# A state-space scan whose decays move from SBUF to PSUM, in one buffer for both channel halves

## The reference, cut to what matters

```python
def step(state, xs):
    d_t, B_t, C_t, u_t = xs
    dA = jnp.exp(d_t[..., None] * A)
    state = state * dA + (d_t * u_t)[..., None] * B_t[:, None, :]
    y_t = jnp.einsum('ben,bn->be', state, C_t)
    return (state, y_t)
...
x = x + jnp.tanh(g_xattn[0]) * _L0_xattn_ref(ctx_1024, _layernorm(x, axis=-1), ...)
x = x + jnp.tanh(g_ffn[0]) * _L0_ffn_ref(_layernorm(x, axis=-1), ...)
x = x + jnp.tanh(g_xattn[1]) * _L1_xattn_ref(ctx_1024, _layernorm(x, axis=-1), ...)
```

## Time and profile before

| | us |
|---|---|
| median of three runs | 1141.84 |
| lowest, highest | 1140.94, 1142.33 |
| profiled execution, its time | 1146.28 |
| profiled execution, span | 1144.1 |
| VectorE busy | 776.8 (68%) |
| TensorE busy | 839.2 (73%) |
| GpSimd busy | 451.9 (39%) |
| ScalarE busy | 379.6 (33%) |

### The profile page before, as it was taken

One profiled execution on the slowest core, in us unless ns is written; L12 is line 12 of the kernel. 1 busy time (PEld: TensorE's weight loads), 2 busy tenths in 40 slices (PEclk: granted clock), 3 DMA queues, 4 the chain that ended last, 5 costly groups with the idle time before them and its releaser, 6 DMA issues.

```text
span 1144.1 us, 12940 instructions
## 1 busy us (share of the span) xinstructions
PE 839.2 (73%) x4202; PEld 522.8 (46%) x4202; DVE 776.8 (68%) x1130; ACT 379.6 (33%) x822; POOL 451.9 (39%) x297
## 2 busy tenths in 40 slices
PE   5797898515676768776739846689985796788993
PEld 2232333313565556554537732444442585555662
DVE  5978999798898889888965583357782835431222
ACT  1623323402333333333335510146553341202331
POOL 3015666003556555655426960033351042151332
PEclk8876888757999999899978978589998998698997
DMA  5102216440212121212010023231313401025113
GB/s 188 41 19 109 71 58 234 194 146 0 74 37 74 37 74 37 73 37 73 0 64 1 1 65 76 36 126 48 111 47 112 136 1 56 0 75 166 46 47 138
DMA packets 28674, 83.77 MB, mean 73 GB/s; under 512 B 3376, under 2 KB 17216, under 8 KB 27104
## 3 DMA queue, kind: packets, MB, share of 16 engines
q1 hardware_dynamic: 26224, 75.35, 20.4%
q0 software_dynamic: 2256, 6.18, 1.5%
q10 hardware_dynamic: 144, 1.57, 0.3%
HBM read 67.74 MB, written 19.45 MB: 76 GB/s over the span
## 4 chain that ended last, share of the span: by engine, by line
PE 42%; DVE 19%; issue 17%; POOL 11%; ACT 5%; DMA 5%; SPq 1%; DVEq 0%; POOLq 0%; ACTq 0%
PE ps L1685 6%; PE ps L511 5%; POOL M L678 5%; PE ps L1331 4%; DVE M L647 3%; PE ps L390 3%; PE ps L504 3%; PE ps L898 2%; PE ps L786 2%; DVE Z L313 2%; POOL ZT L981 2%; PE ps L1350 2%; ACT N L1756 1%; PE ps L1727 1%; DVE stats L305 1%
## 5 line engine op out<-in xcount | busy, mean ns | idle before, releaser
L786 PE MATMUL ps<-W,F 128*128 128x256 f32 x544 | 157.2, 416 | 115.7 <-DVE W L854 82.5
L786 PEld LDWEIGHTS ps<-W,F 128*128 128x128 f32 x544 | 105.8, 204 | 152.4 <-DVE W L854 104.4
L647 DVE TENSOR_TENSOR_SCAN M<-M 128x512 f32<-128x512 f32 x64 | 152.7, 2386 | 21.4 <-POOL M L678 21.4
L685 POOL TENSOR_TENSOR W<-W,M 128x1024 f32<-128x1024 f32 x32 | 75.4, 2356 | 133.6 <-DVE M L655 133.6
L589 POOL TENSOR_TENSOR M<-M 128x1024 f32<-128x1024 f32 x32 | 75.3, 2353 | 100.5 <-DVE M L465 53.6
L818 ACT ACTIVATE F<-ps 128x128 f32<-128x128 f32 x136 | 37.8, 278 | 217.9 <-PE ps L786 217.8
L1756 ACT ACTIVATE N<-ps 128x512 f32<-128x512 f32 x128 | 69.5, 594 | 106.5 <-PE ps L1689 106.5
L1685 PE MATMUL ps<-M,W 32*128 32x256 f32 x512 | 78.9, 440 | 35.3 <-DMA W<-rot_scratch 17.0
L1777 DVE TENSOR_REDUCE W<-ps 128x4 f32<-128x1024 f32 x64 | 78.1, 1221 | 23.9 <-PE ps L1685 16.5
L678 POOL TENSOR_TENSOR M<-N,M 128x1024 f32<-128x1024 f32 x32 | 89.5, 2806 | 0.0
L773 PE MATMUL ps<-W,F 128*128 128x256 f32 x272 | 84.6, 394 | 0.0
(11 more groups left out here) (272 smaller groups left out, 1768.6 us busy)
## 6 DMA issues: line engine op xcount, KB each, us to landing
M<-dbl_scratch SPq DMA_DIRECT2D x48, 512.0 KB, 3.8
W<-in_gu SPq DMA_DIRECT2D x1, 4800.0 KB, 16.3
W<-in_gu SPq DMA_DIRECT2D x1, 4352.0 KB, 14.0
att_scratch<-W SPq DMA_DIRECT2D x32, 128.0 KB
slot_scratch<-in_slots SPq DMA_DIRECT2D x1, 3999.0 KB, 19.0
M<-slot_scratch SPq DMA_DIRECT2D x3, 1032.0 KB, 9.8
W<-in_gu SPq DMA_DIRECT2D x2, 1536.0 KB, 6.9
W<-in_dn SPq DMA_DIRECT2D x1, 2176.0 KB, 18.7
```

Source lines behind the costliest of these rows:

```text
L647: nc.vector.tensor_tensor_scan(hst[:, t, at], dA[:, t, at], dBu[:, t, at], 0.0, ALU.mult, ALU.add).then_inc(S("h1_rdy"), 1)
L685: nc.gpsimd.tensor_tensor(u[1][:, t, :], u[1][:, t, :], hC[:, t, :], ALU.add).then_inc(S("y1_acc"), 1)
L786: last = nc.tensor.matmul(up, ztt[:, par, c, :], gu[:, c, s, :], start=(c == 0), stop=(c == DC - 1))
```

## The change

The second scan reads its decays from PSUM banks 0 and 1 (`dAp1`) instead of SBUF. During this stage only the router has used them before. There is one buffer for both channel halves: bank 0 holds the first half of the tokens, bank 1 the second. ScalarE therefore waits for the scan two pieces before (`g - 1` where it was `g - 3`), and at the start only the pieces of t = 0 need no wait. The zeros at the sequence starts are written to PSUM, after the router's scores have been read. The helper `decay` goes, and the first scan writes out the same operands as before.

```diff
+        dAp1 = ps[:, 0:2, :].rearrange("p a n -> p (a n)")
...
             else:
-                nc.vector.memset(dA.rearrange("p t (b l) -> p t b l", b=BATCH)[:, :, :, 0:1],
-                                 0.0).then_inc(S("delta_done"), 1)
+                dve.wait_ge(S("scores"), 1)
+                nc.vector.memset(dAp1.rearrange("p (b l) -> p b l", b=BATCH)[:, :, 0:1], 0.0).then_inc(S("delta_done"), 1)
...
-                nc.vector.tensor_tensor_scan(hst[:, t, at], dA[:, t, at], dBu[:, t, at], 0.0,
+                nc.vector.tensor_tensor_scan(hst[:, t, at], dAp1[:, at], dBu[:, t, at], 0.0,
                                              ALU.mult, ALU.add).then_inc(S("h1_rdy"), 1)
...
             g = (tile * 4 + 2 * par + t) * 2 + half
-            if not start:
-                act.wait_ge(S("h1_rdy"), g - 3)
-            v, d, _ = decay(0, t, 2 * half, 2 * half + 2)
-            scale = Acur[:, t, par:par + 1]
-            nc.scalar.activation(v, d(1), ACT.Exp, scale=scale).then_inc(S("dA1_rdy"), 1)
+            if not (start and t == 0):
+                act.wait_ge(S("h1_rdy"), g - 1)
+            b = slice(2 * half, 2 * half + 2)
+            nc.scalar.activation(batches(dAp1)[:, b, 1:], batches(delta[1][:, t, :])[:, b, 1:], ACT.Exp,
+                                 scale=Acur[:, t, par:par + 1]).then_inc(S("dA1_rdy"), 1)
```

More of the change, by code:

```diff
@@ L531, in mamba_tail_tensor @@
                 last.then_inc(S("y_tr"), 1)
[L533 to L537, removed]
+        batches = lambda v: v.rearrange("p (b l) -> p b l", b=BATCH)
         def mamba0_scalar(act):
@@ L558, in decays @@
                         act.wait_ge(S("h_rdy"), n * 2 + t)
-                    _, d, scale = decay(n, t, 0, BATCH)
-                    nc.scalar.activation(dAp.rearrange("p (b l) -> p b l", b=BATCH)[:, :, 1:], d(0), ACT.Exp,
+                    scale = Aneg[:, t, n:n + 1] if isinstance(n, int) else Aneg[:, t, bass.ds(n, 1)]
+                    nc.scalar.activation(batches(dAp)[:, :, 1:], batches(delta[0][:, t, :])[:, :, 1:], ACT.Exp,
                                          scale=scale).then_inc(S("dA_rdy"), 1)
```

## The result

The changed kernel takes 1075.64 us at the median of four runs (1071.08 to 1081.59), the kernel before 1142.09 beside it. The ratio is 0.9404, with a 95% interval of 0.9371 to 0.9437. The forecast was 1071.5 us, with a range of 1058 to 1087. The profiled execution took 1076.64 us, its span is 1074.5.

A forecast was written before the change was run, and what follows sets the result against it. VectorE bounds the stage, its second scans and GpSimd's products excluding each other when scan inputs are both in SBUF. Seven tiles at 9.05 plus tile 0's 7.00 give 70.4 us off the 1141.84 median, rounded to 1071.5; range 1058 to 1087.

The forecast's parts named there:

- The scans' held time: Second scan on VectorE: 64 scans at 1.21 us each, so 75.2 of 152.7 us held time goes.
- The tile: One of eight token tiles, 17 expert units each: 29.31 instead of 38.36 us, 9.05 less; tile 0 7.00 less.
- The start with its wait, the unit costs and the two holds: VectorE in tile 4: first scan at 5.03 us; units 1.71 with scan, 1.18 with state product; two 0.68 delays.
- The new wait: State products in units 7 and 11, two SBUF inputs, held until 0.55 us after GpSimd's drive product ends: 0.68 each.
- TensorE: Keeps up from unit 2 if its clock holds; after 2.61 us idle at tile start, the fast level was taken.
- the prediction's alternative: Slow TensorE clock: unit 5 begins at 12.05 not 10.61, unit 7's state product escapes the hold, 0.76 us a tile remains.
- ScalarE's buffer and the memset: Decay waits for the scan two pieces before, always already met; border memset waits for router scores: nothing for either.
- The sum: Whole stage: 7 x 9.05 + 7.00 = 70.4 us less; layers behind it only shift.
- No effect: Rival: scan stays held for its second input and output in SBUF, nothing moves, 1142 us; chance 0.03.
- decay in the path: Rival: single buffer puts ScalarE's decay between scans on 64 pieces, some 55 us given back, 1127 us; chance 0.03.
- GpSimd as the next limit: Rival: sums or drive products come later than walked, 2 to 4 us a tile come back, 1087 to 1103; chance 0.08.
- The slow case: Rival: TensorE at 1.2 GHz for the whole stage, 2.93 us a unit, tile 49.8 us, 1233 us; chance 0.03.

The follow-up runs named there:

- half-and-half kernel: Changed kernel with decays of t = 0 in PSUM banks 0 and 1, those of t = 1 in SBUF, waits as before the change: 1107.37 us, ratio 0.9681.
- pair with small GpSimd products: GpSimd drive products and running sums cut to 8 of 1024 tokens: kernel before (decays in SBUF) 1040.76 us, changed kernel (PSUM) 1040.05 us.
- same reordering: GpSimd makes a tile's first drive product ahead of the previous tile's last running sum: on the changed kernel 1057.29 us, on the kernel before 1137.95 us.

## Why the prediction was right

- **The scans' held time.** Forecast 75.2 us gone and each scan at 1.21, measured 152.7 - 78.0 = 74.7 and 1.22. The half-and-half kernel and the pair with small GpSimd products show the cause: the hold needs both, GpSimd's product and a scan with two inputs in SBUF.
- **The tile.** Forecast 29.31 us, measured 29.34; tile 0 26.68, measured 26.66. The start with its wait, the unit costs and the two holds stand in the timeline as walked.
- **The new wait.** Forecast was a delay of 0.68 twice in a tile, some 16 state products at about 1.4 us. Measured are 1.38 to 1.42 each, ending 0.55 after the drive product's end in the two shown. There are only 12 of them, which the line's total in the stage bears out:

```profile
L652 DVE TENSOR_TENSOR M<-M 128x512 f32<-128x512 f32 x64 | 52.4, 819 | 0.1
```

  (52.4 - 64 x 0.684) / 0.7 is about 12. The four that are missing are those of unit 7 in the four tiles where the clock fell: there it comes after the drive product has ended, or all but ended (0.77 us in the last one), as the prediction's alternative had it.
- **TensorE.** Here the prediction chose wrongly, and it cost little. It took a clock that holds in every tile, because an idle of 2.61 us is nearer to 1.37 than to 4.66, and put 0.76 us on a tile where it does not. It fell in four tiles of seven, in the run made again too. By that price this is 3 us; but the four tiles take 29.27 to 29.53 us (29.39 at the mean) and the three others 29.21 to 29.33 (29.29), so the price is 0.1 us a tile, 0.4 in all. That the stage came out within 0.3 us is therefore owed to the small price and not to the guess. The prediction's sign for it (the matmuls after the wait at 1.1 us mean that the clock held) also misleads in tile 3, where only the next four are slow. In tile 5, which begins at 411.34, the state product of unit 4, unit 5, and the start of the next tile are these:

```profile
421.27 0.68 DVE L652 TENSOR_TENSOR M<-M 128x512 f32<-128x512 f32 x1
...
422.70 0.29 DVE L848 SCALAR_TENSOR_TENSOR F<-F,ps 128x128 f32<-128x128 f32 x1 [0.74 <-ACT F L815]
...
440.73 0.28 DVE L848 SCALAR_TENSOR_TENSOR F<-F,ps 128x128 f32<-128x128 f32 x1
```

  Unit 5 begins at 422.70 and not at 421.27 + 0.60, 0.83 late where 1.44 had been assumed; the hold of unit 7, 0.68, is gone, and the tile takes 29.39 us.
- **ScalarE's buffer and the memset.** Nothing was forecast, and the kernel with one buffer in SBUF shows nothing (0.9987, with 1 inside the interval). The decay got a little shorter, 694 ns instead of about 720, off the path. The memset takes 62 ns where it took 65, with no idle before it, and from its start to the stage's start are 22.25 us where there were 22.28.
- **The sum.** Forecast 70.4 us off the stage, measured 302.23 - 232.07 = 70.16. The first median came out 4 us above the forecast. In the profiled execution the part ahead of the stage was 3.5 us shorter than before (267.26 against 270.74), and the part behind it 4.0 us longer (575.2 against 571.1, spans less the stage's end). The same kernel run again had 571.1 there. So executions scatter by some us outside the stage, for a reason that stays open, and that scatter can account for the first median: the stage of the slower executions wasn't profiled. The second median, 1072.56, is 1.1 from the forecast.

Of the rivals, three don't fit. "No effect" falls with the 64 scans at 1.21 to 1.23 us, and "decay in the path" with ScalarE, which never waits for a scan at a decay. "GpSimd as the next limit" would show scans waiting for the drive product inside a tile; they wait only at its start, seven times. The slow case, a low clock in the whole stage, did not come either: the granted clock over the stage rose from 0.94 to 0.97.

## What to carry to other kernels

When a VectorE instruction of fixed size shows several durations, look at what GpSimd does at those moments: with two SBUF inputs the two exclude each other (every GpSimd instruction here reads SBUF), and one operand in PSUM ends it. Free the operand first and reorder then, since the same reordering was worth 5 us with the decays in SBUF and 15 with them in PSUM. And walk one period of the loop, because a hold that goes lets other instructions meet that never met before.

## What the runs showed of the hardware

Even GpSimd's copy with one SBUF input was held by a scan in the kernel before (its timeline, the copy at the end of tile 4, and the scan beside it):

```profile
451.02 3.00 DVE L647 TENSOR_TENSOR_SCAN M<-M 128x512 f32<-128x512 f32 x1
...
452.87 1.34 POOL L737 COPY F<-ZT 128x256 f32 x1
```

In the changed kernel the same copy is not held, though a scan runs beside it too:

```profile
407.87 1.22 DVE L644 TENSOR_TENSOR_SCAN M<-ps,M 128x512 f32<-128x512 f32 x1
...
408.04 0.40 POOL L734 COPY F<-ZT 128x256 f32 x1
```

1.34 us, ending 0.19 after the scan, against 0.40. So a GpSimd instruction needn't have two inputs to be held by a VectorE instruction that has two in SBUF. Whether one that only writes SBUF is held, or holds, wasn't tried.

In the profiled execution of the changed kernel TensorE's clock fell after idle times of 2.54 (twice), 2.56 and 2.63 us and held after 2.44, 2.61 and 2.62. Run again, it held once after 2.54. So idle of that length doesn't decide it by itself; in the kernel before it fell each time after 4.5 us and more, and held after 1.4 us. It can also fall a little after the engine has started again, as in tile 3. For a forecast such a case has to be carried as open, with a price: here it was 0.1 us a tile.
